# Attention values of a quad of heads as two pieces instead of one

## The chip, the cores and the metric

One NeuronCore of a Trainium2 chip (eight cores) runs the whole kernel. The metric is the time of one execution on the device, in microseconds (us); the median of the runs counts. TensorE multiplies matrices into PSUM, VectorE and ScalarE read PSUM, GpSimd doesn't, and SyncE (SP) issues most DMAs.

## What is computed

x has 2 sequences of 1024 tokens of width 256, the context 2 of 77 tokens. Four steps follow each other, each of them on the normalised output of the one before, gated and added to it:

```python
x = x + jnp.tanh(g_xattn[0]) * _L0_xattn_ref(ctx_1024, _layernorm(x), ...)   # 32 score heads of 8, values 16 heads of 16
x = x + jnp.tanh(g_ffn[0]) * _L0_ffn_ref(_layernorm(x), ...)                 # 3 of 8 zones per sequence, gelu
x = x + jnp.tanh(g_xattn[1]) * _L1_xattn_ref(_layernorm(x), ctx_1024, ...)   # 16 heads of 16, output projection
x = x + jnp.tanh(g_ffn[1]) * _L1_ffn_ref(_layernorm(x), ...)                 # silu(gate) * up, int weights
```

In layer 0 the second softmax of each pair of heads is taken off the first with a learned weight: `att = att[:, :, 0] - lam * att[:, :, 1]`, then `einsum('bhtn,bhnd->bhtd', att, v)`. Layer 1 is plain attention.

## The kernel before

The 2048 tokens are 4 tiles of 512 (J, NT). `plan` writes one list of steps, and every engine walks this same list and emits its own part of each step (the blocks for SP, GpSimd, ScalarE, VectorE and TensorE), with semaphores between them. So the place of a step in the list is its place in each engine's queue.

Attention of one tile works on units of two heads: 16 units in layer 0, 8 in layer 1. "attend" (L1251) is two matmuls with 128 stationary columns (77 of them the context) and 512 moving columns into SC, which has two buffers; ScalarE turns a unit's scores into probabilities with one exponential over 77 x 1024 (L788), into one of four buffers (`probs`). The row maxima are taken off inside the matmul: "max" steps multiply keys and queries for four heads and 128 tokens (L1237) into a bank of AUX (or the spare bank of PV, three banks in turn), VectorE reduces them (L1018), "negmax" transposes them (L1248), ScalarE copies them (L777) and SP moves them with four DMAs into extra rows of the query tile QG (L540), for which the first scores of the next half tile wait (L1255).

"values" works on a quad, that is two units, one quad behind the scores. It multiplies the probabilities by V (77 rows, 17 columns: 16 values and a one for the sum) into the first bank of PV: `attend_values` (L1137). Each product takes one of the four column strips of the array (`PV[32 * r:...]`), so four run at a time; the trace has 16 matmul records of 256 columns for a quad in layer 0 and 32 of 128 columns in layer 1. "outputs" (L1026) is one VectorE transpose of 128 x 512 out of PV into O, which signals `pv_out`; the values of the next quad wait for it (L1144), since this bank of PV has one buffer. "mix" (every second quad) divides by the sums and adds to x on GpSimd.

`attention_tile` (L73) writes the order: after each "attend" of a unit it notes a gap, after every odd unit it puts the oldest quad's "values", a gap, its "outputs" (and "mix"), another gap. `side` steps (norms, query, weight splits, "negmax") stand behind fixed units; fillers (the "max" steps of the next half tile) are then spread evenly over the gaps of a range of units. `attention_end` (L106) adds the last quad. The semaphores around scores and values:

```python
pe.wait_ge(exp_done, n - 1)            # attend of unit n >= 2, L1259
pe.wait_ge(exp_done, 2 * q + 2)        # values of quad q, L1140
pe.wait_ge(pv_out, q)                  # values of quad q >= 1, L1144
act.wait_ge(pv_done, (n - 4) // 2 + 1) # exponential of unit n >= 4, L785
```

By the trace, attention of layer 0 lies between 50 and 194 us, the zones up to 495 us, attention of layer 1 up to 587 us, and the gated step behind it.

Of the kernel before, what the change touches and what calls it, by code (L numbers as in the profile page):

```python
# [31 lines left out]
P = 128  # L32
B, T, D, S = 2, 1024, 256, 77
NT = 512
J = B * T // NT
TT = NT // P
# [4 lines left out]
DV = 16  # L41
# [31 lines left out]
def attention_tile(a, j, side, fillers, left):  # L73

    out, gaps = [], {}

    def gap(u):
        gaps.setdefault(u, []).append(len(out))

    for u in range(HEADS[a] // 2):  # L80
        out.append(("attend", a, j, u))
        gap(u)
        if u % 2:
            if left:
                done = left.pop(0)
                out.append(("values",) + done)
                gap(u)
                out.append(("outputs",) + done)
                if done[2] % 2:
                    out.append(("mix", a, done[1], done[2] // 2))  # L90
                gap(u)
            left.append((a, j, u // 2))
        out += side.get(u, [])
    at = {}
    for filler, first, last in fillers:
        places = [g for u in range(first, last) for g in gaps[u]]
        for i, step in enumerate(filler):
            at.setdefault(places[i * len(places) // len(filler)], []).append(step)
    whole = list(at.get(0, []))
    for i, step in enumerate(out):  # L100
        whole.append(step)
        whole += at.get(i + 1, [])
    return whole


def attention_end(left):  # L106

    out = []
    while left:
        done = left.pop(0)  # L110
        out += [("values",) + done, ("outputs",) + done]
        if done[2] % 2:
            out.append(("mix", done[0], done[1], done[2] // 2))
    return out


def plan():
# [29 lines left out]
    for j in range(J):  # L147
# [23 lines left out]
        if j == 3:  # L171
            spread(side, [("zone_split", 0, f) for f in range(FC // 2)], 10, 16)
        steps += attention_tile(0, j, side, fillers, left)
    steps += attention_end(left)
    steps += [("zone_load2", 0), ("heads", 1, 0), ("heads", 1, 1), ("zone_load", 1), ("zone_load2", 1)]

# [34 lines left out]
    for j in range(J):  # L211
# [26 lines left out]
        if j > 1:  # L238
            norm_in(side, 0, FFN1, j - 2, 1, 1)
        steps += attention_tile(1, j, side, fillers, left)  # L240
    steps += attention_end(left)
    steps += norm(FFN1, 2)
    side = {0: [("scale", FFN1, 2)], 1: [("turn", FFN1, 2)], 3: [("turn_mix", 3)], 5: [("project", 3)],
# [18 lines left out]
def flamingo(nc, x, ctx_t, g_x, g_f, wq0, wk0, wv0, lq1, lq2, lk1, lk2, w1, b1, w2, b2, wa, wb,  # L262
# [24 lines left out]
    with ctx:  # L287
# [6 lines left out]
        def place(name, shape, dt):  # L294
            n = 4
            for s in shape[1:]:
                n *= s
            t = at(name, shape, dt, top[0])
            top[0] += -(-n // 32) * 32
            return t  # L300
# [15 lines left out]
        V = [place(f"V{a}", [P, B, D // DV, DV + 1], F32) for a in range(2)]  # L316
# [95 lines left out]
        PV = ctx.enter_context(nc.psum_tensor("PV", [P, 2, NT], F32))  # L412
        AUX = ctx.enter_context(nc.psum_tensor("AUX", [P, 2, NT], F32))

        def sem(name):
            return ctx.enter_context(nc.semaphore(name))
# [25 lines left out]
        sc_ready, exp_done, pv_done, pv_out = (sem(n) for n in ("sc_ready", "exp_done", "pv_done", "pv_out"))  # L442
# [35 lines left out]
        def unit(a, j, u):  # L478

            return (J * units[0] if a else 0) + units[a] * j + u  # L480

        def probs(n):

            return PB[n % 4] if n % 4 < 2 else PB2[0 if n < A0_UNITS else 1][n % 4 - 2]
# [633 lines left out]
        def _(pe):  # L1118
# [11 lines left out]
            def product(ps, terms, start=True, stop=True):  # L1130

                passes = [p for lh, ll, rh, rl in terms for p in ((lh, rh), (lh, rl), (ll, rh))]
                for i, (lhs, rhs) in enumerate(passes):
                    ins = pe.matmul(ps, lhs, rhs, start=start and i == 0, stop=stop and i == len(passes) - 1)  # L1134
                return ins

            def attend_values(a, j, k):  # L1137

                q = unit(a, j, 0) // 2 + k
                pe.wait_ge(exp_done, 2 * q + 2)  # L1140
                if q == 0:
                    pe.wait_ge(pv_set, 1)
                if q >= 1:
                    pe.wait_ge(pv_out, q)  # L1144
                for i in range(2):
                    p = probs(2 * q + i)[0:S, :, :].rearrange("s i (t q r) -> s i t q r", t=TT, r=32)
                    for n in range(1 if a == 0 else 2):
                        heads = slice(0, 2) if a == 0 else slice(n, n + 1)
                        v = V[a][0:S, j // 2, 2 * k + i if a == 0 else 4 * k + 2 * i + n, :]
                        at_h = P * (2 * i + n)  # L1150
                        for r in range(4):
                            ins = pe.matmul(PV[32 * r:32 * r + DV + 1, 0, at_h:at_h + P * (heads.stop - heads.start)], v,  # L1152
                                            p[:, heads, :, r, :], start=True, stop=True)
                ins.then_inc(pv_done, 1)

            def zone_out(s):

# [28 lines left out]
            for step in PLAN:  # L1186
                kind = step[0]
                if kind == "turn":
                    pe.wait_ge(xn_ready, order[step] + 1)
                    for c in range(KC):  # L1190
                        ps = fill(step + (c,))
                        for t in range(TT):
                            ins = pe.transpose(ps[:, P * t:P * (t + 1)], XN[:, t, P * c:P * (c + 1)], ident[:, :])  # L1193
                        ins.then_inc(aux_ready, 1)
                elif kind == "keys":
                    _, a, i = step
# [6 lines left out]
                    if i < 3:  # L1203
                        for g in range(3 * i, min(3 * i + 3, G)):
                            terms = [(WDH[:, c, g, :, :].rearrange("p q r -> p (q r)"), WDL[:, c, g, :, :].rearrange("p q r -> p (q r)"),
                                      CH[:, c, :], CL[:, c, :]) for c in range(KC)]
                            ins = product(ps[0:ROWS, (g - 3 * i) * B * S:(g - 3 * i + 1) * B * S], terms)
                    else:
                        vh, vl = (WVH, WVL) if a == 0 else (WQ1H, WQ1L)
                        cols = slice((i - 3) * S, (i - 2) * S)  # L1210
                        ins = product(ps[0:S, 0:D], [(CH[:, c, cols], CL[:, c, cols], vh[:, c, :], vl[:, c, :])
                                                     for c in range(KC)])
                    ins.then_inc(aux_ready, 1)
                elif kind == "query":
                    _, a, j = step
# [9 lines left out]
                elif kind == "max":  # L1225

                    _, a, j, t, u = step
                    n = J * a + j
# [5 lines left out]
                    for i in range(4 // NS[a]):  # L1234
                        g = u * (4 // NS[a]) + i
                        n_cols = NS[a] * S
                        ins = pe.matmul(ps[:, i * n_cols:(i + 1) * n_cols], QG[n % 2][0:ROWS, g, P * t:P * (t + 1)],  # L1237
                                        KA[a][0:ROWS, j // 2, NS[a] * g:NS[a] * (g + 1), :].rearrange("p h n -> p (h n)"),
                                        start=True, stop=True)
                    ins.then_inc(aux_ready, 1)  # L1240
                elif kind == "negmax":
                    _, a, j, c = step
# [4 lines left out]
                    for t in range(TT):  # L1247
                        ins = pe.transpose(ps[0:n_heads, P * t:P * (t + 1)],  # L1248
                                           NM[:, (J * a + j) % 2, t, n_heads * c:n_heads * (c + 1)], ident[:, :])
                    ins.then_inc(aux_ready, 1)  # L1250
                elif kind == "attend":  # L1251
                    _, a, j, u = step
                    n, m = unit(a, j, u), J * a + j
# [8 lines left out]
                    for i in range(2):  # L1262
                        h = 2 * u + i
                        at_h = (j // 2 * HEADS[a] + h) * S
                        ins = pe.matmul(SC[:, n % 2, i, :], KALL[a][:, at_h:at_h + P], QG[m % 2][:, h // NS[a], :],  # L1265
                                        start=True, stop=True)
                    ins.then_inc(sc_ready, 1)
                elif kind == "values":
                    attend_values(*step[1:])
                elif kind == "route" and step[2] == 0:  # L1270
                    b = step[1]
# [6 lines left out]
                    for i, (c, j) in enumerate(cols):  # L1278
                        ins = pe.matmul(ps[0:RH, 0:1], W1[:, c, :], POOLED[:, c, j:j + 1], start=i == 0, stop=i == len(cols) - 1)
                    ins.then_inc(aux_ready, 1)  # L1280
                elif kind == "route":
# [3 lines left out]
                              start=True, stop=True).then_inc(aux_ready, 1)  # L1285
                elif kind == "zone":
                    s = step[1]
                    z, nt, f = s // PER, s % PER // FC, s % FC
                    j = 2 * (z // TOPK) + nt
# [18 lines left out]
                elif kind == "out":  # L1308
                    pe.wait_ge(ys_ready, order[step] + 1)
                    for i in range(2):  # L1310
                        ps = fill(step + (i,))
                        for t in (2 * i, 2 * i + 1):
                            for c in range(KC):
                                at_c = D * (t % 2) + P * c
                                ins = pe.transpose(ps[:, at_c:at_c + P], YS[:, c, P * t:P * (t + 1)], ident[:, :])
                        ins.then_inc(aux_ready, 1)
                elif kind == "turn_mix":
                    j = step[1]
                    for c in range(KC):
                        pe.wait_ge(mixed, oct_of(1, j, c) + 1)  # L1320
                        ps = fill(step + (c,))
                        for t in range(TT):
                            ins = pe.transpose(ps[:, P * t:P * (t + 1)], MIX[:, t, P * c:P * (c + 1)], ident[:, :])
                        ins.then_inc(aux_ready, 1)
                elif kind == "project":
                    j = step[1]
# [3 lines left out]
                    for i in range(2):  # L1330
                        ps = fill(step + (i,))
                        for t in (2 * i, 2 * i + 1):
                            rows = slice(P * t, P * (t + 1))
                            ins = product(ps[:, D * (t % 2):D * (t % 2 + 1)],
                                          [(XH[:, j, k, rows], XL[:, j, k, rows], WOH[:, k, :], WOL[:, k, :]) for k in range(KC)])
                        ins.then_inc(aux_ready, 1)
                elif kind == "gated":
                    s = step[1]
                    j, f = divmod(s, HC)
# [9 lines left out]
                    for i, (wh, wl) in enumerate(((WGH, WGL), (WUH, WUL))):  # L1349
                        ins = product(SC[:, s % 2, i, :], [(wh[:, c, cols], wl[:, c, cols], XH[:, j, c, :], XL[:, j, c, :])  # L1350
                                                           for c in range(KC)])
# [53 lines left out]
```

## Time and profile before

| what | value |
|---|---|
| runs | 702.23, 705.49, 706.5 us; median 705.49 |
| the profiled execution | 702.88 us, span 701.1 us, 10175 instructions |
| busy, share of the span | TensorE 90%, its weight loads 69%, VectorE 52%, ScalarE 53%, GpSimd 18% |
| mean granted clock of TensorE | 0.945 of full |

The span runs from the first to the last instruction of one profiled execution. Busy is the sum of the durations of an engine's instructions with overlaps merged; the ends of matmuls are modelled, so that a busy TensorE is not one at its peak. In the rows PE is TensorE, PEld its weight loads, DVE VectorE, ACT ScalarE, POOL GpSimd. A granted clock of 1.0 is 2.4 GHz, 0.5 is 1.2 GHz; a mean in between says how long either was granted. L1152 is line 1152 of the kernel.

### The profile page before, as it was taken

What the parts mean: (1) busy time and instruction counts of PE and PEld (TensorE: products, weight loads), DVE (VectorE), ACT (ScalarE), POOL (GpSimd) and SP (SyncE); (2) the same over time, 40 slices, a digit from 0 to 9 for tenths busy, and PEclk for the clock granted to TensorE, in tenths of its full rate; (3) what the DMA queues carried; (4) which work ended last, traced back from release to release, by engine and by line L of the source; (5) the groups of instructions that cost most, each with busy time, mean ns of one, the idle gap of its engine ahead of it and who ended that gap; (6) DMA issues with size and microseconds to landing.
All of it is one profiled execution on the core that took longest, in us unless ns stands there. A gap on an engine that the chain in (4) does not pass through costs nothing.

```text
span 701.1 us, 10175 instructions
## 1 busy us (share of the span) xinstructions
PE 633.0 (90%) x3676; PEld 483.5 (69%) x3676; DVE 367.2 (52%) x814; ACT 369.3 (53%) x627; POOL 127.4 (18%) x182
## 2 busy tenths in 40 slices
PE   2699888887799999999999999999877979999996
PEld 2575555554478788888888787778566757888884
DVE  6677667777473523425446445443456665443332
ACT  4326747564865745646657445445753755243232
POOL 8433355253630000000000000001112213000000
PEclk9769999999889999999999999999997799999999
DMA  7321120112013030110302330000161100000000
GB/s 224 94 71 25 33 64 2 47 47 93 1 36 115 2 121 0 58 63 1 121 22 69 86 125 2 2 0 2 38 201 35 47 4 1 1 30 1 30 31 30
DMA packets 22354, 34.67 MB, mean 49 GB/s; under 512 B 4640, under 2 KB 13216, under 8 KB 22304
## 3 DMA queue, kind: packets, MB, share of 16 engines
q1 hardware_dynamic: 20800, 32.09, 15.2%
q0 software_dynamic: 1216, 1.87, 1.3%
q8 instruction: 29, 0.48, 0.3%
q14 instruction: 21, 0.17, 0.1%
q10 hardware_dynamic: 288, 0.07, 0.1%
HBM read 18.93 MB, written 2.10 MB: 30 GB/s over the span
## 4 chain that ended last, share of the span: by engine, by line
PE 75%; DVE 7%; ACT 5%; SPq 4%; issue 4%; POOL 3%; DMA 2%; ACTq 0%; DVEq 0%; POOLq 0%
PE SC L1134 28%; PE PV L1134 26%; PE AUX L1134 4%; PE PV L1152 4%; PE SC L1265 4%; PE AUX L1237 4%; SPq L529 2%; DVE NM L1018 2%; PE AUX L1193 2%; SPq L540 2%; DMA QG<-NMT 2%; DVE O L1026 1%; ACT XN L736 1%; PE PV L1237 1%; POOL QG L639 1%
## 5 line engine op out<-in xcount | busy, mean ns | idle before, releaser
L878 DVE TENSOR_TENSOR HL<-HF,HH 128x512 fp32r<-128x512 f32 x120 | 83.3, 694 | 157.3 <-ACT HH L830 157.1
L788 ACT ACTIVATE PB<-SC 77x1024 f32<-77x1024 f32 x96 | 94.6, 1014 | 56.5 <-PE SC L1265 56.4
L830 ACT ACTIVATE HH<-PV 128x512 fp32r<-128x512 f32 x96 | 57.3, 596 | 67.1 <-PE SC L1134 67.1
L825 ACT ACTIVATE HF<-PV 128x512 f32<-128x512 f32 x96 | 57.3, 597 | 58.3 <-PE PV L1134 56.2
L1265 PE MATMUL SC<-QG,KA 128*128 128x512 f32 x192 | 71.8, 467 | 13.9 <-DMA QG<-NMT 11.4
L1134 PE MATMUL PV<-XH,WAH 128*128 128x512 f32 x192 | 78.7, 410 | 1.0 <-DVE O L1026 1.0
L613 POOL TENSOR_TENSOR RSTD<-RSTD,NHALF 128x4 f32<-128x4 f32 x16 | 17.8, 1110 | 333.7 <-DVE RSTD L949 333.7
L1134 PE MATMUL PV<-XL,WAH 128*128 128x512 f32 x192 | 76.8, 400 | 0.0
L1134 PE MATMUL PV<-XH,WAL 128*128 128x512 f32 x192 | 76.7, 399 | 0.0
L1134 PE MATMUL SC<-HL,WBH 128*128 128x512 f32 x192 | 75.6, 394 | 0.0
L1134 PE MATMUL SC<-HH,WBH 128*128 128x512 f32 x192 | 75.3, 392 | 0.0
L1134 PE MATMUL SC<-HH,WBL 128*128 128x512 f32 x192 | 75.0, 390 | 0.0
L1018 DVE TENSOR_REDUCE NM<-AUX 128x4 f32<-128x308 f32 x142 | 62.8, 464 | 14.0 <-PE AUX L1237 14.0
L1237 PE MATMUL AUX<-KA,QG 96*128 96x154 f32 (+1 forms) x198 | 53.3, 341 | 10.1 <-DVE NM L1018 5.8
L1237 PEld LDWEIGHTS AUX<-KA,QG 96*128 96x128 f32 x198 | 38.9, 216 | 28.6 <-DVE NM L1018 13.3
L1152 PE MATMUL PV<-PB,V 77*17 77x256 f32 (+1 forms) x1024 | 56.2, 354 | 2.5 <-DVE O L1026 2.5
L1265 PEld LDWEIGHTS SC<-QG,KA 128*128 128x128 f32 x192 | 35.0, 216 | 22.9 <-DMA QG<-NMT 13.4
L859 ACT ACTIVATE SG<-SC 128x512 f32<-128x512 f32 x24 | 14.3, 597 | 68.4 <-PE SC L1134 68.4
L1109 DVE SCALAR_TENSOR_TENSOR HF<-SC,SG 128x512 f32<-128x512 f32 x24 | 16.6, 692 | 60.6 <-ACT SG L859 60.6
L1026 DVE STREAM_TRANSPOSE O<-PV 128x512 f32<-128x512 f32 x48 | 34.1, 710 | 21.2 <-PE PV L1152 21.1
L1152 PEld LDWEIGHTS PV<-PB,V 77*17 77x17 f32 x1024 | 26.5, 104 | 25.4 <-issue 11.3
L1134 PEld LDWEIGHTS PV<-XH,WAH 128*128 128x128 f32 x192 | 36.8, 192 | 8.9 <-issue 1.5
(238 smaller groups left out, 1198.8 us busy)
## 6 DMA issues: line engine op xcount, KB each, us to landing
QG<-QH SPq DMA_DIRECT2D x112, 64.0 KB, 2.0
WSA<-in_wa SPq DMA_DIRECT2D x6, 1024.0 KB, 5.0
WSB<-in_wb SPq DMA_DIRECT2D x12, 512.0 KB, 6.6
QG<-QL SPq DMA_DIRECT2D x56, 64.0 KB, 2.0
X<-in_x SPq DMA_DIRECT2D x4, 512.0 KB, 6.4
out_x<-X SPq DMA_DIRECT2D x4, 512.0 KB, 2.6
QG<-QH POOLq DMA_DIRECT2D x16, 64.0 KB, 2.3
WI<-in_wg SPq DMA_DIRECT2D x1, 768.0 KB, 4.4
```

The lines of the kernel that those rows point to most:

```text
L613: pool.tensor_tensor(RSTD[:, 1, :], RSTD[:, 0, :], NHALF[:, :], ALU.pow).then_inc(pool_step, 1)
L788: act.activation(probs(n)[0:S, :, :], SC[0:S, n % 2, :, :], ACT.Exp, scale=SCALE[a]).then_inc(exp_done, 1)
L825: act.activation(HF[s % 2][:, :], PV[:, s % 2, :], ACT.Gelu_apprx_tanh)
L830: act.activation(HH[s % 2][:, :], PV[:, s % 2, :], ACT.Gelu_apprx_tanh).then_inc(act_done, 1)
L878: return dve.tensor_tensor(dst, raw, hi.bitcast(F32), ALU.subtract)
L1018: dve.tensor_reduce(NM[:, n % 2, t, 4 * u:4 * u + 4], bank(key)[:, 0:4 * S].rearrange("p (h n) -> p h n", h=4), AX_X, ALU.max, negate=True ...
L1026: dve.transpose(O[q // 2 % 2][:, 4 * (q % 2):4 * (q % 2) + 4, :, :].rearrange("p h t d -> p (h t d)"), PV[:, 0, :]).then_inc(pv_out, 1)
L1109: dve.scalar_tensor_tensor(HF[s % 2][:, :], SC[:, s % 2, 1, :], DEQ, SG[s % 2][:, :], ALU.mult, ALU.mult).then_inc(hf_ready, 1)
L1134: ins = pe.matmul(ps, lhs, rhs, start=start and i == 0, stop=stop and i == len(passes) - 1)
L1152: ins = pe.matmul(PV[32 * r:32 * r + DV + 1, 0, at_h:at_h + P * (heads.stop - heads.start)], v, p[:, heads, :, r, :], start=True, stop=True)
L1237: ins = pe.matmul(ps[:, i * n_cols:(i + 1) * n_cols], QG[n % 2][0:ROWS, g, P * t:P * (t + 1)], KA[a][0:ROWS, j // 2, NS[a] * g:NS[a] * (g ...
L1265: ins = pe.matmul(SC[:, n % 2, i, :], KALL[a][:, at_h:at_h + P], QG[m % 2][:, h // NS[a], :], start=True, stop=True)
```

## The change

The step ("values", a, j, k) gets a fourth number i, 0 or 1, and makes only the products of one of the quad's two units. In `attention_tile` piece 0 comes after the even unit's scores and piece 1 after the odd unit's; each is followed by a gap for fillers. Piece i waits for the exponential of its own unit, both for the transpose of the quad before, and only piece 1 signals `pv_done`. "outputs" and "mix" stay behind the odd unit. Side steps of an even unit now stand behind piece 0. The fillers' places are counted over more gaps.

```diff
--- before.py
+++ after.py
@@ -80,15 +80,16 @@
     for u in range(HEADS[a] // 2):
         out.append(("attend", a, j, u))
         gap(u)
-        if u % 2:
-            if left:
-                done = left.pop(0)
-                out.append(("values",) + done)
-                gap(u)
+        if left:
+            done = left[0]
+            out.append(("values",) + done + (u % 2,))
+            gap(u)
+            if u % 2:
+                left.pop(0)
                 out.append(("outputs",) + done)
                 if done[2] % 2:
                     out.append(("mix", a, done[1], done[2] // 2))
-                gap(u)
+        if u % 2:
             left.append((a, j, u // 2))
         out += side.get(u, [])
     at = {}
@@ -108,7 +109,7 @@
     out = []
     while left:
         done = left.pop(0)
-        out += [("values",) + done, ("outputs",) + done]
+        out += [("values",) + done + (0,), ("values",) + done + (1,), ("outputs",) + done]
         if done[2] % 2:
             out.append(("mix", done[0], done[1], done[2] // 2))
     return out
@@ -1134,24 +1135,24 @@
                     ins = pe.matmul(ps, lhs, rhs, start=start and i == 0, stop=stop and i == len(passes) - 1)
                 return ins
 
-            def attend_values(a, j, k):
+            def attend_values(a, j, k, i):
 
                 q = unit(a, j, 0) // 2 + k
-                pe.wait_ge(exp_done, 2 * q + 2)
+                pe.wait_ge(exp_done, 2 * q + i + 1)
                 if q == 0:
                     pe.wait_ge(pv_set, 1)
                 if q >= 1:
                     pe.wait_ge(pv_out, q)
-                for i in range(2):
-                    p = probs(2 * q + i)[0:S, :, :].rearrange("s i (t q r) -> s i t q r", t=TT, r=32)
-                    for n in range(1 if a == 0 else 2):
-                        heads = slice(0, 2) if a == 0 else slice(n, n + 1)
-                        v = V[a][0:S, j // 2, 2 * k + i if a == 0 else 4 * k + 2 * i + n, :]
-                        at_h = P * (2 * i + n)
-                        for r in range(4):
-                            ins = pe.matmul(PV[32 * r:32 * r + DV + 1, 0, at_h:at_h + P * (heads.stop - heads.start)], v,
-                                            p[:, heads, :, r, :], start=True, stop=True)
-                ins.then_inc(pv_done, 1)
+                p = probs(2 * q + i)[0:S, :, :].rearrange("s i (t q r) -> s i t q r", t=TT, r=32)
+                for n in range(1 if a == 0 else 2):
+                    heads = slice(0, 2) if a == 0 else slice(n, n + 1)
+                    v = V[a][0:S, j // 2, 2 * k + i if a == 0 else 4 * k + 2 * i + n, :]
+                    at_h = P * (2 * i + n)
+                    for r in range(4):
+                        ins = pe.matmul(PV[32 * r:32 * r + DV + 1, 0, at_h:at_h + P * (heads.stop - heads.start)], v,
+                                        p[:, heads, :, r, :], start=True, stop=True)
+                if i:
+                    ins.then_inc(pv_done, 1)
 
             def zone_out(s):
```

## Rows read from the trace of the kernel before

**Rows 1.** Stretches: start:end, length, busy us (instructions) of PE, PEld, DVE, ACT, POOL, PEclk, DMA, GB/s

```profile
54.00:81.00 27.00, 23.46 (x182) 13.80 (x175) 17.59 (x44) 17.17 (x23) 9.90 (x14) 0.94 0.07 18
81.00:125.00 44.00, 37.51 (x287) 24.11 (x286) 29.56 (x80) 27.83 (x44) 20.89 (x29) 0.96 0.16 39
125.00:159.00 34.00, 28.67 (x221) 16.45 (x219) 27.16 (x70) 21.30 (x31) 15.18 (x24) 0.95 0.20 49
159.00:194.00 35.00, 27.88 (x205) 15.16 (x205) 21.67 (x50) 23.18 (x34) 16.10 (x24) 0.84 0.14 47
...
495.00:587.00 92.00, 77.49 (x805) 59.65 (x806) 55.40 (x122) 53.34 (x67) 21.66 (x18) 0.85 0.23 62
```

**Rows 2.** The chain that ended last, shares by engine, then by line

```profile
PE 75%; DVE 7%; ACT 5%; SPq 4%; issue 4%; POOL 3%; DMA 2%; ACTq 0%; DVEq 0%; POOLq 0%
```

**Rows 3.** Costliest groups: values (busy us, mean ns | idle before, releaser)

```profile
L1152 PE MATMUL PV<-PB,V 77*17 77x256 f32 (+1 forms) x1024 | 56.2, 354 | 2.5 <-DVE O L1026 2.5
```

**Rows 4.** Timeline of TensorE, dense stretch, tile 2 (start, length, engine, line)

```profile
131.79 0.41 PE L1237 MATMUL AUX<-KA,QG 96*128 96x308 f32 x1
132.13 1.06 PE L1152 MATMUL PV<-PB,V 77*17 77x256 f32 x16
133.12 0.41 PE L1237 MATMUL PV<-KA,QG 96*128 96x308 f32 x1
133.36 0.45 PE L1237 MATMUL AUX<-KA,QG 96*128 96x308 f32 x2
...
134.34 0.63 PE L1265 MATMUL SC<-QG,KA 128*128 128x512 f32 x2
134.81 0.32 PE L1237 MATMUL AUX<-KA,QG 96*128 96x308 f32 x1
134.96 0.64 PE L1265 MATMUL SC<-QG,KA 128*128 128x512 f32 x2
135.53 1.06 PE L1152 MATMUL PV<-PB,V 77*17 77x256 f32 x16
```

**Rows 5.** Timeline of VectorE, the same stretch

```profile
133.56 0.48 DVE L1018 TENSOR_REDUCE NM<-PV 128x4 f32<-128x308 f32 x1 [0.67 <-PE PV L1237]
133.96 0.47 DVE L1018 TENSOR_REDUCE NM<-AUX 128x4 f32<-128x308 f32 x1
134.34 0.71 DVE L1026 STREAM_TRANSPOSE O<-PV 128x512 f32<-128x512 f32 x1
```

**Rows 6.** Timeline of TensorE, bare stretch, layer 1

```profile
507.00 1.07 PE L1152 MATMUL PV<-PB,V 77*17 77x128 f32 x32
507.99 1.36 PE L1265 MATMUL SC<-QG,KA 128*128 128x512 f32 x4
509.28 1.07 PE L1152 MATMUL PV<-PB,V 77*17 77x128 f32 x32
```

**Rows 7.** Timeline of VectorE, the same stretch

```profile
508.13 0.72 DVE L1026 STREAM_TRANSPOSE O<-PV 128x512 f32<-128x512 f32 x1 [1.01 <-PE PV L1152]
```

**Rows 8.** Who TensorE waited for: us in total, times, longest

```profile
PE SC L1265 <- DMA QG<-NMT: 11.4, 6, 3.1
PE AUX L1237 <- DVE NM L1018: 5.8, 8, 3.6
...
PE PV L1152 <- DVE O L1026: 2.5, 2, 2.3
...
PE SC L1265 <- ACT PB L788: 2.3, 3, 2.0
...
PE PV L1248 <- DVE NM L1018: 1.7, 2, 1.2
```

**Rows 9.** Stretches, columns as in rows 1: tile 3's end; first half of tile 2

```profile
184.00:191.10 7.10, 5.25 (x52) 1.92 (x40) 5.85 (x13) 7.08 (x13) 6.41 (x11) 1.00 0.00 0
125.40:136.50 11.10, 10.07 (x77) 5.51 (x75) 8.79 (x21) 5.84 (x7) 2.74 (x4) 1.00 0.29 71
```

**Rows 10.** Timeline of ScalarE, layer 1

```profile
513.21 1.48 ACT L851 ACTIVATE WGH<-WI 128x1536 fp32r<-128x1536 int32 x1 [2.51 <-DMA WI<-in_wg]
```

## The prediction

> **What bounds the kernel now.** I read the stages first. In the table of stretches [rows 1] the four attention tiles of layer 0 take 27, 44, 34 and 35 us and the attention of layer 1 takes 92 us; TensorE is busy 80 to 87% of each by modelled ends, VectorE 60 to 80%. No engine is full. The change works only there, in 232 of 701 us. Over the whole span the chain that ended last is 75% TensorE [rows 2], but most of that is the zone and gated stages, which the change leaves alone. So in attention any nanosecond put on TensorE's queue counts until TensorE next waits for something that was not itself delayed. The costliest groups give the count of matmuls of values, 1024 of 0.35 us with the gap before them put down to the transpose in 2.5 us alone [rows 3]; they are 48 quads. Then two closer looks at the timeline: a dense stretch [rows 4, 5] and a bare one [rows 6, 7]. Last, what TensorE waits for [rows 8], and where something other than TensorE sets the pace [rows 9, 10].
>
> **What the change says, and what it can give.** `values` waits for an exponential. Before the values of quad q stands ("attend", 2q+3), which itself waits until `exp_done` is 2q+2, exactly what the values ask. The new first piece asks for 2q+1 and stands behind attend 2q+2, which has already waited for 2q+1. So in both orders the exponential is there when the values come, and splitting the wait saves nothing; only the last quad of each attention, in `attention_end`, differs, and it stands behind the transpose of the quad before it (part of the 2.5 us over 2 waits in [rows 8]) in either order. TensorE waits for exponentials ahead of scores in 3 places, 2.3 us in all [rows 8]: half a block of values moved between the two scores can fill such a wait, but little is there to fill.
>
> **Part 1, another switch per quad.** In [rows 4], scores to maximum is 134.81 - 134.34 = 0.47 us, scores to values 135.53 - 134.96 = 0.57: the way in costs 0.10, from a maximum more (132.13 - 131.79 = 0.34 against 134.96 - 134.81 = 0.15 from a maximum to scores, 0.19). The 16 matmuls of a quad lie in four rounds; (1.06 - 0.38)/3 = 0.23 us each by the width of the group less one matmul (0.38 being what one of them takes, an estimate from the 0.35 mean of [rows 3] and the 0.39 to 0.41 of its neighbours), so 0.91 of the 0.99 from 132.13 to 133.12 is work and 0.08 the way out. The maximum that follows takes 133.36 - 133.12 = 0.24 instead of 0.15: 0.09. One visit to the 77x17 form thus costs 0.27 to 0.36 us over its work; I take 0.33. The change adds one per quad, except in the last quad of each attention, whose pieces stand together: 46 x 0.33 = 15 us if nothing hides it.
>
> The Trainium skill speaks of this: "TensorEngine Tiling (Array Packing)", section Key Properties, says that changing the tiling mode drains TensorE, and "TensorE: Matmul & The Clock Gate", Part 2, puts the drain at some 128 cycles. At 2.4 GHz that is 0.053 us, twice per visit, an estimate of 4.9 us for the 46; this case's rows show three times that, since the weights behind the switch aren't loaded ahead either, and I go by the rows.
>
> **Part 2, the wait for the transpose comes one unit earlier.** PV has one buffer; the values of the next quad need `pv_out` of this one. Up to now two scores stand between, now one. Bare case [rows 6, 7]: values at 507.00, scores at 507.99, transpose 508.13 to 508.85, 0.86 after the scores began. In the new order the first piece would be ready 0.57 after them and so waits about 0.3. Period now 509.28 - 507.00 = 2.28; new: second piece 0.55, scores 0.57, wait 0.3, first piece 0.55, scores 0.57, second piece again: 2.6 to 2.7, so +0.4. Behind the waiting piece stand the next scores, and for them ScalarE.
>
> **Part 3, the maxima are spread over more gaps.** `gap` is now called twice in an even unit and three times in an odd one (once and three times before), so fillers come in ones more often. Two walks, with the durations above, three banks for the maxima, 0.41 us (0.30 when streaming) from a maximum's issue to its end, 0.39 between reductions in a row and 0.71 for a transpose [rows 4, 5, 7].
> Dense quad (one maximum per gap, units 6 to 13): second piece at 0, maximum 0.55, maximum 0.80, scores 0.94, maximum 1.40, first piece could start at 1.7. VectorE: reduction 1.0 to 1.45, transpose to 2.15, so the piece starts at 2.2; maximum 2.77, scores 3.0, maximum 3.5, second piece 3.8. The same stretch takes 135.53 - 132.13 = 3.40 now [rows 4]: +0.4 a quad.
> First half of a tile (units 0 to 5, 16 maxima, three quads): now 11.10 us from the first scores to the transposed maxima, with 8.79 of VectorE [rows 9] and an idle 0.67 behind each block of values, since TensorE feeds VectorE nothing meanwhile [rows 5]. In the new order a maximum follows each half block; the waits for the transpose (0.7 and 0.3) take about what that starving and one wait for a bank give back. The walk ends at 11.0. I count 0, three tiles long.
>
> **Which quads pay.** Layer 0, 32 quads. Dense, 0.4 each: quads 2, 3, 4 of tile 0, quad 3 of tile 1, quads 4, 5 of tile 2: 2.4 us. Few maxima, partly beside ScalarE, 0.35 each: quads 0, 1, 6 of tile 0, 4 and 6 of tile 1, 3 of tile 3: 2.1. First halves (9 quads): 0. Hidden (10 quads): those before the first scores that wait for the moved maxima (6 such waits, 11.4 us, the longest 3.1, [rows 8]), those before a normalised tile, and quads 4 to 6 of tile 3, where ScalarE is busy 7.08 of 7.10 us [rows 9]. The last: 0. Sum 4.5.
> Layer 1, 16 quads. The first five are hidden: ScalarE stands idle 2.51 us until the gate weights land at 513.21 [rows 10], and that DMA goes by SP's own queue. Four are in first halves: 0, since there the transposed maxima wait for VectorE as it is (1.7 us over 2 waits, [rows 8]). Six pay 0.42; among them the ones at unit 6 of tiles 1 and 2, where the first piece now stands ahead of `negmax`, so that the maxima leave some 0.4 us later for a chain (copy, four DMAs on SP, next scores) that ends in the longest DMA wait, 3.1 us. The last: 0. Sum 2.5.
> No instruction is added for VectorE, ScalarE, GpSimd or SP; SP and GpSimd only see their steps later.
> Together 7.0 us. The profiled execution took 702.88 us (span 701.1 and 1.8 around it), so 709.9; the median of the runs is 2.6 above the profiled one, so 712.5. If cover is gone everywhere, 46 quads at 0.4 to 0.5 are 18 to 23 us; if every piece is hidden, nothing.
>
> **Rivals.**
> Cover is thin: the waits I count as hiding are themselves pushed back, as when a piece moves ahead of the maxima that start their chain. For it: the drains are certain, TensorE is busy over 80%, and the granted clock (0.84 to 0.96 of full in attention, [rows 1]) may fall further with more breaks; at half clock each term nearly doubles. Against: the six long DMA waits. Some 35 quads paying 0.45: +16, 721.
> All hidden: the split does not do what it says (the exponential was there anyway), and drains vanish in waits. +1, 706.5. For it: VectorE and ScalarE are busy 60 to 80% and each covers gaps of TensorE.
> It gets faster: in the dense quads VectorE, not TensorE, is the pace, and the half blocks end its starving, 0.67 us a quad [rows 5]. TensorE's own waits for reductions ahead of maxima are small (5.8 us over 8, [rows 8]), but the gap is on VectorE's side; if over 15 of the 31 quads with maxima nearby get 0.67 back while the wait for the transpose costs nothing beyond the switch (-0.67 + 0.33), it is -5: 700.5. It decides from the point where the transpose is done before the first piece comes; against it stands the reduction that is queued ahead of the transpose in each dense quad.
>
> **Chances.** Forecast (+4 to +12) 0.50; thin cover 0.15; all hidden 0.25; faster 0.10. A measurement of this kernel tells about 1%, 7 us, from no change. The forecast lies on that line: half of it above, half below. Slower by over 1%: 0.25 + 0.15 and a little for a slow tail, 0.43; within: 0.46; faster: 0.11. Range 701 to 721; the likeliest case's own is 709 to 717.
>
> **What would show it.** Right: values in half blocks of 8 matmuls, 0.55 us from the first to whatever follows; issue gaps ahead of values nearly twice as many; a new wait of values for the transpose of 0.2 to 0.6 us in most dense quads; first halves of tiles still 11 us; tile 0 longer by about 2 us; zone stage unchanged; no value piece that waits for an exponential. Wrong: dense quads at 3.4 us or less, or tiles 1 to 3 longer by over 2 us each, or a lower granted clock in attention that carries most of the difference.

## The result and the profile after

The change makes the kernel slower: 732.1 us as the median of four runs (722.93 to 732.46) beside 706.0 us before, a ratio of 1.035 (95% interval 1.026 to 1.044), so 26 us. Forecast were 7 us, with a range of 701 to 721 us. The profiled execution has a span of 730.4 us and a mean granted clock of 0.908 (before: 701.1 us and 0.945).

The first thing to look at are the slices of the page's second part that give the granted clock, one digit for a fortieth of the span, in tenths; first the kernel before:

```profile
PEclk9769999999889999999999999999997799999999
```

And the changed one:

```profile
PEclk9779989955589999999999999999796599999999
```

The three slices at 5 are TensorE at or close to 1.2 GHz. The stretches of the changed kernel, columns as in [rows 1], cut where the same transpose stands in both kernels, and behind them the stretch that is at half clock from end to end:

```profile
54.00:146.30 92.30, 77.97 (x569) 44.75 (x568) 63.23 (x156) 55.64 (x77) 36.44 (x51) 0.94 0.14 33
146.30:214.00 67.70, 60.84 (x318) 28.32 (x317) 35.06 (x90) 36.49 (x54) 25.12 (x41) 0.60 0.12 36
512.00:616.00 104.00, 87.52 (x809) 61.65 (x809) 55.51 (x120) 55.50 (x68) 23.07 (x18) 0.79 0.20 55
```

```profile
145.40:189.70 44.30, 43.45 (x196) 21.66 (x195) 24.05 (x63) 19.43 (x27) 12.37 (x22) 0.50 0.19 55
```

The same cut of the kernel before:

```profile
54.00:141.90 87.90, 75.53 (x574) 46.23 (x567) 61.47 (x156) 54.31 (x77) 36.60 (x51) 0.96 0.14 35
141.90:194.00 52.10, 42.00 (x318) 23.30 (x316) 34.50 (x89) 35.17 (x54) 25.47 (x40) 0.86 0.16 46
```

Up to the transpose at 146.3 (141.9 before) the clocks are nearly alike, 0.94 and 0.96, and the change has cost 4.4 us. In the rest of layer 0's attention it costs another 15.6 at 0.60 against 0.86; this is where most of the time went. VectorE's and ScalarE's busy times hardly move (35.06 and 36.49 against 34.50 and 35.17), so they had no more to do: TensorE is slower and they wait. The third row is layer 1, at 0.79 against 0.85 in [rows 1]. Its edges are round numbers; from its first scores to its last values it takes 612.26 - 514.03 = 98.2 us, where before it took 582.93 - 495.55 = 87.4, so 10.9 us more. The stages between and behind took the same time as before within 1.3 us.

The dense stretch of tile 0 in the changed kernel, TensorE, answers to [rows 4]:

```profile
59.99 0.30 PE L1238 MATMUL AUX<-KA,QG 96*128 96x308 f32 x1
60.22 0.63 PE L1152 MATMUL PV<-PB,V 77*17 77x256 f32 x8
60.78 0.41 PE L1238 MATMUL AUX<-KA,QG 96*128 96x308 f32 x1
61.03 0.62 PE L1266 MATMUL SC<-QG,KA 128*128 128x512 f32 x2
61.49 0.30 PE L1238 MATMUL PV<-KA,QG 96*128 96x308 f32 x1
62.48 0.63 PE L1152 MATMUL PV<-PB,V 77*17 77x256 f32 x8 [0.69 <-DVE O L1027]
...
63.97 0.63 PE L1152 MATMUL PV<-PB,V 77*17 77x256 f32 x8
...
66.61 0.63 PE L1152 MATMUL PV<-PB,V 77*17 77x256 f32 x8 [0.91 <-ACT PB L789]
```

VectorE beside it answers to [rows 5]:

```profile
61.23 0.48 DVE L1019 TENSOR_REDUCE NM<-AUX 128x4 f32<-128x308 f32 x1 [0.42 <-PE AUX L1238]
61.62 0.71 DVE L1027 STREAM_TRANSPOSE O<-PV 128x512 f32<-128x512 f32 x1
...
65.76 0.71 DVE L1027 STREAM_TRANSPOSE O<-PV 128x512 f32<-128x512 f32 x1
```

A half block takes 60.78 - 60.22 = 0.56 us to whatever follows, and a quad, second piece to second piece, 63.97 - 60.22 = 3.75. The first piece at 62.48 waits 0.69 us for the transpose, which ends at 62.33. TensorE stood ready at 62.48 - 0.69 = 61.79. The transpose could have started with the end of the second piece's last matmul, 60.22 + 0.63 = 60.85, and started at 61.62: VectorE's queue has the maximum that TensorE issued behind that piece (60.78) in front of it. The wait at 66.61 is put down to an exponential. It is the transpose again: 65.76 + 0.71 = 66.47 lies 0.14 before the piece, as 62.33 lies 0.15 before 62.48, and the exponential that this piece asks for was needed by the scores ahead of it. The only other wait of values with this name, 0.91 us at 134.53, is of the same kind: there the transpose ends at 134.38. The name belongs to something that ended at about the same moment, so a wait on several semaphores is to be checked by its distances.

Who TensorE waited for in the changed kernel, columns as in [rows 8]:

```profile
PE PV L1152 <- DVE O L1027: 15.6, 20, 2.0
...
PE SC L1266 <- DMA QG<-NMT: 12.1, 5, 4.5
...
PE SC L1266 <- ACT PB L789: 2.0, 1, 2.0
PE PV L1152 <- ACT PB L789: 1.8, 2, 0.9
```

Values waited 2.5 us for the transpose before and wait 15.6 us now, 17.4 with the two misnamed ones. The wait for exponentials ahead of scores went from 2.3 to 2.0: little was there to win, and 0.3 us were won.

### The profile page after: what moved, and what is told of

Same layout as the page of the kernel before. It is cut to its first block, busy times and chain, and to the rows that moved or that the text cites. A ratio compares the mean times of both kernels' runs of the same rounds, so it can differ in the third digit from the quotient of the medians.

```text
span 730.4 us, 10223 instructions
## 1 busy us (share of the span) xinstructions
PE 662.6 (91%) x3676; PEld 487.6 (67%) x3676; DVE 368.1 (50%) x814; ACT 373.3 (51%) x627; POOL 129.1 (18%) x182
## 3 DMA queue, kind: packets, MB, share of 16 engines
q1 hardware_dynamic: 20800, 32.09, 14.5%
## 4 chain that ended last, share of the span: by engine, by line
PE 78%; DVE 7%; ACT 4%; issue 3%; SPq 3%; DMA 2%; POOL 2%; ACTq 0%; DVEq 0%; POOLq 0%
PE SC L1135 27%; PE PV L1135 25%; PE PV L1152 7%; PE SC L1266 5%; PE AUX L1135 4%; PE AUX L1238 4%; SPq L530 2%; PE AUX L1194 2%; DVE O L1027 2%; DVE NM L1019 2%; PE PV L1238 2%; SPq L541 1%; DMA QG<-NMT 1%; ACT XN L737 1%; POOL QG L640 1%
## 5 line engine op out<-in xcount | busy, mean ns | idle before, releaser
L789 ACT ACTIVATE PB<-SC 77x1024 f32<-77x1024 f32 x96 | 97.1, 1016 | 68.9 <-PE SC L1266 68.5
L1266 PE MATMUL SC<-QG,KA 128*128 128x512 f32 x192 | 82.3, 518 | 14.0 <-DMA QG<-NMT 12.1
L1152 PE MATMUL PV<-PB,V 77*17 77x256 f32 (+1 forms) x1024 | 73.9, 394 | 17.6 <-DVE O L1027 15.6
L614 POOL TENSOR_TENSOR RSTD<-RSTD,NHALF 128x4 f32<-128x4 f32 x16 | 17.4, 1090 | 329.8 <-DVE RSTD L950 329.8
L1238 PE MATMUL AUX<-KA,QG 96*128 96x154 f32 (+1 forms) x195 | 56.0, 355 | 4.4 <-ACT NMT L778 2.4
L1238 PEld LDWEIGHTS AUX<-KA,QG 96*128 96x128 f32 x195 | 40.4, 225 | 28.9 <-issue 14.7
L1152 PEld LDWEIGHTS PV<-PB,V 77*17 77x17 f32 x1024 | 23.1, 105 | 53.6 <-issue 36.4
L1266 PEld LDWEIGHTS SC<-QG,KA 128*128 128x128 f32 x192 | 38.6, 240 | 26.0 <-DMA QG<-NMT 14.6
```

Of the source, the lines that this page charges most:

```text
L614: pool.tensor_tensor(RSTD[:, 1, :], RSTD[:, 0, :], NHALF[:, :], ALU.pow).then_inc(pool_step, 1)
L789: act.activation(probs(n)[0:S, :, :], SC[0:S, n % 2, :, :], ACT.Exp, scale=SCALE[a]).then_inc(exp_done, 1)
```

## The experiments

The theories: (a) the clock, that more breaks on TensorE let its granted clock fall; (b) the wait for the transpose, now a unit earlier; (c) the extra visit to the 17-column form. The rival to all is (d) the order of the maxima or the split wait itself. The "order of before" in the diffs is `gap` after the odd unit's values and after its "outputs".

**The split wait alone.** Both pieces behind the odd unit, with the gaps of before.

```diff
...
+        if u % 2:
+            if left:
+                done = left.pop(0)
+                out += [("values",) + done + (0,), ("values",) + done + (1,)]
+                gap(u)
                 out.append(("outputs",) + done)
...
+                gap(u)
```

> Two pieces with a wait each, but side by side behind the odd unit, fillers in the old gaps: no extra switch, no earlier wait for the transpose, no other order. If the loss comes from where the pieces stand (switches, transpose, order, and the clock that follows from them), this is the kernel before: 702 to 708 us, ratio 0.99 to 1.01. If splitting the step and its wait costs by itself (one more wait on TensorE per quad), some 48 x 0.05 to 0.1 = 2 to 5 us more.

Measured: 706.19 us, ratio 1.001 (0.998 to 1.004). Splitting the step costs nothing and gains nothing within 0.4%, so the loss comes from where the pieces stand.

**The order alone.** Values whole; the maxima in the gaps of the changed kernel.

```diff
-        if u % 2:
-            if left:
+        if left:
+            if u % 2:
                 done = left.pop(0)
                 out.append(("values",) + done)
+            gap(u)
...
```

> Values whole behind the odd unit as before, but the maxima in the gaps as the changed kernel counts them (two in every unit, none behind the transpose). Only the order differs. If the order of the maxima (more of them ahead of the transpose on VectorE) carries a good part of the 26 us, this is 710 us or more. If the switches and the earlier wait carry it, 700 to 709 us, with the granted clock near 0.94.

Measured: 704.5 us, ratio 0.998 (0.995 to 1.001). The order by itself is harmless, so (d) falls for whole values; the next run shows that the order matters once the pieces wait.

**The transpose ahead of the maximum.** The changed kernel, with the odd unit's second gap behind "outputs".

```diff
             out.append(("values",) + done + (u % 2,))
-            gap(u)
             if u % 2:
                 left.pop(0)
                 out.append(("outputs",) + done)
...
+            gap(u)
```

> The changed kernel, but the gap of the odd unit stands behind the transpose, not ahead of it, so that a maximum is no longer queued on VectorE between the second piece and its transpose. If the wait of the next first piece for the transpose is the main loss, it shrinks by about 0.4 us in some 20 quads and the time falls by 8 us or more, to 724 or below, and the clock with it if the waits bring it down. If the switches are the main loss, the time stays within 3 us of the changed kernel's 732.

Measured: 720.87 us, ratio 1.019 (1.013 to 1.025), so 11 of the 26 us are back. Values wait for the transpose 7.5 us in 9 places, not 15.6 in 20. The same dense stretch:

```profile
60.04 0.63 PE L1152 MATMUL PV<-PB,V 77*17 77x256 f32 x8
...
61.60 0.63 PE L1152 MATMUL PV<-PB,V 77*17 77x256 f32 x8
...
63.09 0.63 PE L1152 MATMUL PV<-PB,V 77*17 77x256 f32 x8
```

```profile
60.73 0.72 DVE L1027 STREAM_TRANSPOSE O<-PV 128x512 f32<-128x512 f32 x1
```

The transpose starts at 60.73, the first piece at 61.60 waits for nothing that the profile names, and the quad takes 3.05 us: 0.70 less than in the changed kernel. That is less than the 3.40 of [rows 4] too, but that quad lies in another tile and holds five maxima, not four. The same quad in the run on the order alone, whole values with four maxima, is the fair comparison:

```profile
59.09 1.06 PE L1153 MATMUL PV<-PB,V 77*17 77x256 f32 x16
...
61.79 1.06 PE L1153 MATMUL PV<-PB,V 77*17 77x256 f32 x16
```

It takes 2.70 us. So with the transpose in time the half blocks cost 0.35 us in this quad, about one visit, and no gain for VectorE is seen. The next quad, five maxima in both, takes 66.24 - 63.09 = 3.15 against 64.85 - 61.79 = 3.06. The clock of the profiled run is 0.908 as in the changed kernel, that of the other three 0.916 to 0.920: on (a) the run doesn't decide.

**More work, the same waits.** The changed kernel, with one scores matmul of each even unit made twice. The output is the same.

```diff
+                        for _ in range(2 if u % 2 == 0 and i == 0 else 1):
-                        ins = pe.matmul(SC[:, n % 2, i, :], ...)
+                            ins = pe.matmul(SC[:, n % 2, i, :], ...)
```

> The changed kernel, with the first scores matmul of every even unit made twice into the same place (the second overwrites the first, nothing else changes): 48 more matmuls of 0.23 us, 11 us of work at full clock, in front of the piece that waits for the transpose. If the waits and the clock are the loss, the work fits into the wait and keeps TensorE busier: 725 to 735 us, with a granted clock above 0.91. If TensorE is the bound throughout and the clock has nothing to do with its gaps, 739 to 745 us with the clock at 0.905 or less.

Measured: 719.68, 721.31, 732.66 and 736.04 us, with clocks of 0.941, 0.941, 0.919 and 0.913. The runs are spread too wide for a ratio. The first two are faster than all four runs of the changed kernel, with 11 us more of work in them; the other two are no faster than its slower ones. In all of them the time goes with the clock. So does the changed kernel's own: its run at 722.93 had 0.925, the other three 0.903 to 0.908. This agrees with (a) and proves nothing by itself.

**Two buffers for the values.** First the base, whole values that take turns in PV's two banks, with two banks left for the maxima; then the change on it.

```diff
-    home, uses, turn_now, banks, lent = {}, [0, 0, 0], 0, 3, []
+    home, uses, turn_now, banks, lent = {}, [0, 0, 0], 0, 2, []
...
-                                  PV[:, 0, :]).then_inc(pv_out, 1)
+                                  PV[:, q % 2, :]).then_inc(pv_out, 1)
...
-                if q >= 1:
-                    pe.wait_ge(pv_out, q)
+                if q >= 2:
+                    pe.wait_ge(pv_out, q - 1)
...
-                            ins = pe.matmul(PV[32 * r:32 * r + DV + 1, 0, at_h:at_h + P * (heads.stop - heads.start)], v,
+                            ins = pe.matmul(PV[32 * r:32 * r + DV + 1, q % 2, at_h:at_h + P * (heads.stop - heads.start)], v,
...
```

> A base for the next one: the kernel before with two buffers for the values (quads take turns in PV's two banks) and only two banks left for the maxima and the other products. The values of a quad wait for the transpose of the quad before last. Fewer banks for the maxima cost something in the dense stretches: 706 to 722 us.

> The same two buffers, with the change. The first piece no longer waits for the transpose of the quad just before. If that wait is the main part of the loss, this is within 8 us of its base, the two-buffer kernel with whole values, and no wait of values for the transpose is left. If the switches alone cost what the rows of before say (0.33 us each, half of them hidden) it is 7 us above its base at the same clock, and 15 us or more where the clock falls as well.

Measured: 732.72 us (1.038, 1.032 to 1.044) and 732.83 us (1.037, 1.031 to 1.043). The base missed its range: taking the third bank from the maxima costs some 26 us, the second buffer for the values notwithstanding. On this base the change costs 0.1 us, extra visits included (the two intervals leave room for some 5 us either way), and neither kernel has a wait of values for the transpose. This speaks for (b), with a reserve: maxima waited for VectorE 14.9 us in 27 places in the base and 7.7 in 14 in the other, so that a visit can hide here that could not otherwise.

**One more visit and nothing else.** Adjacent pieces, with one 128x128 transpose of the identity between them, into columns that the second piece writes over.

```diff
...
                 if i:
                     ins.then_inc(pv_done, 1)
+                else:
+                    pe.transpose(PV[:, 0, 2 * P:3 * P], ident[:, :], ident[:, :])
```

> Both pieces side by side behind the odd unit, with one transpose of 128x128 between them (into columns that the second piece overwrites; what it leaves in rows that nobody reads stays). So every quad has one more visit to the 17-column form and nothing else is moved: 48 x (0.33 + 0.11) us = 21 us if TensorE is the bound everywhere, 8 to 12 us if half of it is hidden as the prediction has it: 714 to 718 us, clock near 0.935. If the switches are what brings the clock down, more than 722 us with a clock under 0.92.

Measured: 715.83 us, ratio 1.014 (1.009 to 1.018), at clocks of 0.934 to 0.938. The forecast for "half of it hidden" was met, and the visits leave the clock alone: (c) costs some 10 us here, the added transposes included, and isn't what slows the clock.

**The wait alone.** Values whole, order of the changed kernel, and TensorE waits for `pv_out` behind the even unit's scores, where the first piece would stand.

```diff
+            else:
+                out.append(("wait_out",) + left[0])
             gap(u)
...
+                elif kind == "wait_out":
+                    q = unit(step[1], step[2], 0) // 2 + step[3]
+                    if q >= 1:
+                        pe.wait_ge(pv_out, q)
```

> Values whole behind the odd unit and the order of the changed kernel (as in the run on the order alone), but TensorE waits for the transpose of the quad before at the place where the first piece would stand. No extra switch. If the earlier wait is the main loss, this is 715 to 728 us with a clock under 0.93, and with the 9 us of the visit alone it makes up the changed kernel's 26. If only both together cost (the wait alone is filled, since the scores of the even unit have run anyway), it is 705 to 711 us.

Measured: 718.18 us (710.28 to 719.32), ratio 1.013 (1.007 to 1.019), three runs at clocks of 0.915 to 0.920 and the fastest at 0.933. Against the order alone, which has the same steps but the wait, that is over 1% for a wait that adds no instruction of an engine, and the clock fell. In the profiled run TensorE waits 14.5 us for the transposes of attention, at most 2.1 at a time; the waits for the moved maxima are 11.1 us, at most 3.8 at a time (13.2 and 3.5 with the order alone).

**Holding the clock.** Eight matmuls of 512 columns ahead of the first scores of each half tile from the second tile on, where TensorE waits for the moved maxima; the scores overwrite what they write. The same edit on whole values, on the changed kernel, on the changed kernel with the transpose first, on the wait alone and on the visit alone; and with four matmuls on whole values.

```diff
                     if u % (units[a] // KC) == 0:
+                        if n >= 2:
+                            pe.wait_ge(exp_done, n - 1)
+                        if n > 8:
+                            for _ in range(8):
+                                pe.matmul(SC[:, n % 2, 0, :], KALL[a][:, 0:P], KALL[a][:, 0:NT], start=True, stop=True)
                         pe.wait_ge(m_moved[m % 2][u // (units[a] // KC)], ...)
```

> The kernel before, with eight score-like matmuls of 0.23 us ahead of the first scores of each half tile from the second tile on, where TensorE stands waiting for the moved maxima; they write a buffer that the scores overwrite. 13 places x 1.85 us = 24 us of work. If the granted clock falls because TensorE waits there, it rises to 0.95 or more and the time is 697 to 706 us in spite of the added work; if the clock has another cause, it is 708 to 722 us with the clock at 0.94.

> The changed kernel with the eight matmuls ahead of the first scores of each half tile. On whole values these took the clock from 0.94 to 0.965 and left the time as it was. If the long stretch at half clock in tiles 2 and 3 is the second half of the loss, and work in the waits prevents it, this is 712 to 724 us with a clock of 0.94 or more. If the clock follows from the many short breaks at the values and not from the long waits, it stays near 0.91 and the time goes to 732 to 745 us.

> The changed kernel with both mendings: the transpose ahead of the maximum on VectorE (alone 721 us at a clock of 0.908) and the eight matmuls. What is left at a good clock is the cost of the switches and of the rest of the wait: 707 to 714 us at 0.95 or more if these two account for all but the switches; above 718 us if not.

> The earlier wait for the transpose alone (no extra switch; alone 718 us at a clock of 0.915), with the eight matmuls that held the clock at 0.965. If the wait costs mostly by way of the clock, this is 704 to 709 us at 0.96, next to whole values with the same eight matmuls (706). If it costs by its own length, 710 to 718 us.

> The extra visit alone (one 128x128 transpose between two adjacent pieces; alone 716 us at 0.936), with the eight matmuls. The visit showed no fall of the clock, so its 9 to 10 us should stay: 713 to 718 us at 0.96. If it falls to 709 or below, the visit too cost partly by the clock.

> Whole values with four instead of eight matmuls ahead of the first scores of each half tile: half the added work, so less of it stands beyond the wait. If a part of the clock's gain stays (0.95 or more), 699 to 704 us, a kernel faster than before; if it goes, 704 to 709 us.

| kernel | without, us (clock of the profiled run) | with eight matmuls, us (clock) | ratio of these to the kernel before |
|---|---|---|---|
| whole values | 706.0 (0.945) | 706.05 (0.959) | 0.999 (0.996 to 1.002) |
| the change | 732.1 (0.908) | 712.7 (0.965) | 1.009 (1.006 to 1.012) |
| the change, transpose first | 720.87 (0.908) | 706.08 (0.963) | 0.999 (0.996 to 1.001) |
| the wait alone | 718.18 (0.915) | 705.77 (0.973) | 0.999 (0.996 to 1.001) |
| the visit alone | 715.83 (0.936) | 716.56 (0.963) | 1.012 (1.009 to 1.015) |

The changed kernel with the eight matmuls: the clock's slices, and its waits.

```profile
PEclk9779999996989999999999999999999999999999
```

```profile
PE PV L1152 <- DVE O L1027: 15.5, 18, 2.4
...
PE PV L1152 <- ACT PB L789: 4.7, 5, 1.0
...
PE SC L1271 <- DMA QG<-NMT: 3.0, 4, 1.2
```

The waits for the transpose are all still there, 15.5 us, and yet 19 us are gone: most of the loss came by the clock. The wait alone shows it cleanest: 12 us with the clock falling, and nothing with the eight matmuls, though TensorE waits 17.1 us for the transposes there. The visit is the other way round: 10 us at either clock. In the changed kernel a part does go by length. Between its two rows with the eight matmuls only one gap is moved, the waits of values for the transpose fall from 15.5 to 6.6 us, and the time falls by 6.6.

"Held" is said of the mean clock, and the stages differ. The stretches between the first, the 19th and the last transpose of layer 0, and between the first and the last of layer 1, first for whole values with the eight matmuls, then for the changed kernel with them:

```profile
53.15:144.65 91.50, 82.14 (x586) 52.17 (x585) 61.53 (x155) 53.83 (x77) 36.70 (x51) 0.93 0.14 34
144.65:195.87 51.22, 43.88 (x338) 24.20 (x336) 33.44 (x88) 34.97 (x54) 25.53 (x40) 0.95 0.16 47
505.58:588.87 83.29, 77.42 (x805) 60.52 (x806) 49.07 (x97) 47.60 (x61) 19.39 (x15) 0.92 0.24 68
```

```profile
54.92:147.06 92.14, 79.06 (x585) 47.22 (x584) 63.08 (x155) 55.35 (x77) 36.50 (x51) 0.98 0.14 34
147.06:205.67 58.61, 50.02 (x338) 25.23 (x336) 33.60 (x87) 35.85 (x54) 25.41 (x40) 0.86 0.13 41
515.06:596.37 81.31, 75.79 (x805) 55.89 (x806) 47.73 (x98) 48.47 (x61) 22.27 (x15) 0.99 0.25 70
```

What the change still costs sits in the middle row, 7.4 us, and there the clock is 0.86 against 0.95; layer 1 has the better clock and is 2.0 us shorter. So neither the 19 us of the clock nor the 7 us of the rest is a clean figure; the changed kernel's rest still has some clock in it.

Four matmuls on whole values: 703.56 us, ratio 0.9965 (0.994 to 0.999), 0.35% faster than the kernel before and the lowest median of this study, with 704.5 of the order alone close by.

## Why the prediction was wrong

What was right. The split of the wait gives nothing, as the thresholds in the code said, and no piece is seen to wait for an exponential (the two waits with that name are the transpose's). The wait for the transpose is there, and the issue gaps of weight loads ahead of values went from 35 to 63, nearly twice as many. The half block is 0.56 us (forecast 0.55), a dense quad 3.75 (forecast 3.8). Up to 146 us, at nearly equal clocks, the sum says 3.4 us (tile 0, tile 1 and the first half of tile 2) and the cut gives 4.4, though not in the parts foretold: from its first to its last transpose tile 0 is 0.9 us longer (30.28 to 31.17), not 2, and to the last of tile 1 it is 2.7 more. And with the eight matmuls in both kernels the change costs 712.7 - 706.05 = 6.7 us, where the sum said 7.0. That agreement is luck: the 6.7 sits in tiles 2 and 3 at a lower clock, and the terms came out otherwise, as below. The prediction also named the sign that it would be wrong by, a lower granted clock in attention that carries most of the difference, and that sign came.

What failed:

1. The step that failed is the granted clock. The sum was made at the clocks of the kernel before; a fall stood only as an argument for the rival with thin cover, which was priced at 721 and given 0.15. Some 19 of the 26 us go with that fall (732.1 against 712.7, with the waits in place in both, while the same eight matmuls leave whole values at 706). The prediction had the means to see that this matters: [rows 1] shows 0.84 to 0.96 in the attention stages (the zones, 194 to 495 us, have 0.99), so attention was below full already, and at half clock a half block takes 0.99 us (149.82 to 150.81 in the changed kernel), not 0.56.
2. Part 2, the wait. 17.4 us in 22 places, 0.79 each, not 0.3 to 0.5. For whole values its length is covered, as the wait alone with the eight matmuls shows (705.77 us); in the changed kernel some of it isn't (712.7 against 706.08 with the transpose first). What it does to the clock had no price. The bare case was also added up wrongly: 0.55 + 0.57 + 0.3 + 0.55 + 0.57 is 2.54, so 0.26 more than 2.28, not 0.4. The trace has 530.99 - 528.20 = 2.79 us for such a quad in layer 1, 0.5 more: the way from scores to a piece took 0.67, not 0.57, and the wait was 0.28.
3. Part 3 counted the gaps wrongly: an odd unit has two in the changed code, not three, and none behind the transpose. The walk put one maximum ahead of the transpose in each dense quad and so met the true order there all the same; but it missed that the gap behind the transpose was gone. Putting it back takes 11 us off the changed kernel, and 6.6 with the eight matmuls in both.
4. Part 1, the visit. Alone it costs 10 us with its own transpose of some 0.11 us, out of the 21 that the rows gave, so half hidden, as assumed. Inside the change it may cost less: with the transpose first and the eight matmuls, the change has all its extra visits and is at 706.08, level with whole values at 706.05. Why isn't shown. The third rival's gain, half blocks that end VectorE's starving once the transpose is done before the first piece comes, is not seen in the dense quad above (3.05 us against 2.70 for whole values in the same order), and no run has whole values in that order together with the eight matmuls.

What stays open. The clock was raised by work in the long DMA waits, and those eight matmuls take time of their own (some 1.85 us at 14 places, not 13 as the expectations say; part of it beyond the wait), so that comparison is between kernels that both carry them. Which waits the clock answers to isn't shown either: the earlier wait for the transpose lowers it, but with the DMA waits filled it is up again while the waits for the transpose stay. And why the clock stayed low for just 44 us from 145.3 on in the profiled run isn't shown: TensorE was busy 43.45 of these 44.30 us by modelled ends, at half clock.

## What to carry to other kernels

Before a change puts a wait in front of TensorE, look at the granted clock of the stage: here, where it was already below full, a wait whose length was hidden still cost 12 us through the clock, and the experiment that showed it was to fill the long waits with spare matmuls. Where two halves of a block share one output buffer, the instruction that empties it has to stand first on its engine, ahead of work that is only convenient there. And count an order written by a program from the code as it will be, line by line, since here the place of one gap was worth 11 us.

## What was not expected of the hardware

Added work made a kernel faster. The changed kernel with eight more matmuls at 14 places got 19 us faster, and two of four runs with 48 more matmuls beat all of its runs. The granted clock fell to one half for 44 us on end while TensorE was busy 98% of them by modelled ends; before that stretch, from 100 to 145.3 us, it was busy 37.93 of 45.30 us at a mean clock of 0.89, with no wait ahead of a matmul longer than 1.99 us:

```profile
100.00:145.30 45.30, 37.93 (x267) 22.98 (x267) 30.55 (x78) 25.49 (x40) 16.48 (x26) 0.89 0.13 33
```

The Trainium skill, "TensorE: Matmul & The Clock Gate", section HAM oscillation — how this bites in real kernels, ties such a fall to waits for DMA in which TensorE idles, and advises to order the loop so that it stays busy. That the eight matmuls in the DMA waits took the clock from 0.91 to 0.965 agrees. What these runs add: extra switches of form don't lower the clock (0.936 against 0.94), and earlier waits for the transpose of at most 2.1 us do (0.915 for the wait alone, 0.936 for its order without it), in a run whose DMA waits of up to 3.8 us are hardly longer than the 3.5 without them.
